# Moving the deferred second half of the output epilogue behind the first block of the Wo projection

## The chip, the cores and the metric

The kernel runs as one program on the eight cores of one Trainium2 chip. Each core takes half of the sequence of one of four batch entries; the cores exchange nothing. The metric is the device time of the slowest core in microseconds (us), as the median of the runs.

## The reference

One recurrent layer over x of shape (4, 4096, 2048): a layernorm, a linear attention with grouped keys and values, a feed-forward net with sign weights, and a gated sum.

```python
def recurrent_layer(x, ...):
    xn = _layernorm(x, axis=-1)
    # attention: q, k, v projections; sq, sk = elu + 1; per head
    kv = jnp.einsum('bhsd,bhse->bhde', sk, v)
    qkv = jnp.einsum('bhsd,bhde->bhse', sq, kv)
    k_sum = sk.sum(axis=2)
    norm = jnp.einsum('bhsd,bhd->bhs', sq, k_sum)
    s = (qkv / (norm[..., None] + EPS))...reshape(b, s, H * D) @ Wo.T
    # feed-forward with sign weights
    hidden = relu(einsum('bsd,hd->bsh', xn, sign(up_weight)) * up_scale)
    out = einsum('bsh,dh->bsd', hidden, sign(down_weight)) * down_scale * output_scale
    return x + s * silu(out)
```

## The kernel before

A first phase normalises the sequence, builds the small attention state and stores converted weights to DRAM. The second phase, `phase_c`, runs over four token blocks of 512 tokens (`tau` 0 to 3). A block has four stages, and TensorE goes through them in this order:

1. Q and attention: 16 heads, `emit_q` (L608) and `emit_attn_tail` (L648 to L688). The last instruction is VectorE's product into `attn_t` (L688).
2. Wo: eight output blocks `ntb` of 256 columns, each with four groups `sub` of 128 tokens. A group is 16 matmuls (L742) into one of only two PSUM buffers, `PS[6]` and `PS[7]`, and one evacuation by ScalarE into `s_tile` (L752). Group number `gidx = 4*ntb + sub`; group g waits for the evacuation of group g-2 (L735 to L739). The weights of a block, 1024 KB, come by a DMA issued on GpSimd's queue (`emit_wo_load`, L715). There are two weight buffers, so the load for block n+2 waits for the last group of block n (L714), and it is emitted at the end of block n.
3. Up: 64 blocks of 16 matmuls (L817), evacuated by ScalarE (L823); weights come by GpSimd's queue (L806).
4. Down: two halves of 1024 output columns (L875, L919, L965), each followed by an epilogue made in `_dn_evac`.

The epilogue has eight pieces i = 0 to 7 of 128x512. The evacuation to `t1_all` (L1030) is made at once. `phase2a` is silu (L1041) and the product with `s_tile` (L1047). `phase2b` adds the residual rows of x and stores the result: for each piece, VectorE's sum into `yt` (L1060), GpSimd's store DMA (L1067), and then, on ScalarE's queue, the load of the x rows of piece i+3 (`emit_xr_load`, L1014 to L1016). Buffers tie these together. `xr` has three slots, so the load for piece i+3 waits for sum i; `yt` has two, so sum i waits until the store of piece i-2 has landed (L1058 to L1059).

For the first half of the columns both parts run at once. For the second half they are kept for the next block: `phase2a` is emitted in front of head 2 of the next Q stage (L694 to L697), and `phase2b` is `pending_ph2b`, emitted after the loads of Wo blocks 0 and 1 and ahead of the first Wo group (L721 to L723). This happens in blocks tau 1, 2 and 3; tau 0 has nothing pending, and that of the last block runs at the very end (L986 to L989).

Each engine executes its instructions in program order, with waits on counting semaphores in the same stream. A DMA is issued by an engine (SP, ScalarE or GpSimd), in order with everything else on that engine. So where `pending_ph2b` is emitted sets its place in three streams: VectorE's, ScalarE's and GpSimd's.

```python
W("vector", S[f"XR{r['slot']}"], r["xr_done"])
if self.yw_done[p4]:
    W("vector", S[f"YW{p4}"], self.yw_done[p4])
... sum L1060, then
W("gpsimd", S["VE"], S["VE"].v)
... store L1067, then
if i + NXR < 8:
    emit_xr_load(i + NXR)     # W("scalar", S["VE"], xr_free[slot]); DMA on ScalarE's queue
```

Of the kernel before, what the change touches and what calls it, by code (L numbers as in the profile page):

```python
# [41 lines left out]
class Builder:  # L42
# [25 lines left out]
    def W(self, eng, sem, v=None):  # L68
        if v is None:
            v = sem.v  # L70
        if v <= 0:
            return
        self.prog.emit(eng, lambda e, h=sem.h, v=v: e.wait_ge(h, v))

    def OP(self, eng, fn, *incs):
        pairs = []
        for s, n in incs:
            s.v += n
            pairs.append((s.h, n))

        def cl(e, fn=fn, pairs=pairs):
            inst = fn(e)
            for h, n in pairs:
                inst = inst.then_inc(h, n)

        self.prog.emit(eng, cl)
# [398 lines left out]
    def phase_c(self, scope):  # L485
# [101 lines left out]
        for tau in range(NTC):  # L587
# [120 lines left out]
            def emit_wo_load(ntb):  # L708
                osl = ntb % 2
                wo = S[f"WO{osl}"]  # L710
                prevs = s_pe.get((tau, ntb - 2, 3)) if ntb >= 2 else (
                    s_pe.get((tau - 1, NTB - 2 + ntb, 3)) if tau >= 1 else None)
                if prevs:
                    W("gpsimd", S["PE"], prevs)  # L714
                OP("gpsimd", lambda e, d=wo_sl[osl], n=ntb: e.dma_start(  # L715
                    d[:], D["woS"][n, :, :]), (wo, 16))
                wo_done[ntb] = wo.v

            emit_wo_load(0)
            emit_wo_load(1)  # L720
            if getattr(self, "pending_ph2b", None) is not None:  # L721
                self.pending_ph2b()
                self.pending_ph2b = None  # L723
            for ntb in range(NTB):
                osl = ntb % 2
                W("tensor", S[f"WO{osl}"], wo_done[ntb])
                if ntb == 0:
                    W("tensor", S["VE"], attn_done_ve)
                    if tau >= 1:
                        W("tensor", S["VE"], self.dn_evac_ve[6])  # L730
                        W("tensor", S["VE"], self.dn_evac_ve[7])
                for sub in range(4):
                    gidx = ntb * 4 + sub
                    psl = PS[6 + (gidx % 2)]
                    war = s_evac_se.get((tau, gidx - 2)) if gidx >= 2 else (  # L735
                        s_evac_se.get((tau - 1, NTB * 4 - 2 + gidx)) if tau >= 1
                        else None)
                    if war:
                        W("tensor", S["SE"], war)  # L739
                    for h in range(H):  # L740
                        OP("tensor", lambda e, h=h, sub=sub, p=psl, w=wo_sl[osl]:
                           e.matmul(p[:, 0:256],  # L742
                                    attn_t[:, h * 512 + sub * 128:
                                           h * 512 + (sub + 1) * 128],
                                    w[:, h * 256:(h + 1) * 256],
                                    start=(h == 0), stop=(h == H - 1)),
                            *(((S["PE"], 1),) if h == H - 1 else ()))
                    s_pe[(tau, ntb, sub)] = S["PE"].v
                    W("scalar", S["PE"], S["PE"].v)
                    if gidx == 0 and tau >= 1:  # L750
                        W("scalar", S["VE"], self.last_stile_ve)
                    OP("scalar", lambda e, sub=sub, n=ntb, p=psl: e.copy(  # L752
                        s_tile[:, sub * DM + n * 256: sub * DM + (n + 1) * 256],
                        p[:, 0:256]), (S["SE"], 1))
                    s_evac_se[(tau, gidx)] = S["SE"].v
                if ntb + 2 < NTB:
                    emit_wo_load(ntb + 2)
            s_pe[(tau, "end")] = S["PE"].v

            if tau == 1:  # L760
# [377 lines left out]
```

How the kernel before makes its waits and increments, by code:

```python
    def W(self, eng, sem, v=None):  # L68
        if v is None:
            v = sem.v
        if v <= 0:
            return
        self.prog.emit(eng, lambda e, h=sem.h, v=v: e.wait_ge(h, v))
# [7 lines left out]
        def cl(e, fn=fn, pairs=pairs):  # L81
            inst = fn(e)
            for h, n in pairs:
                inst = inst.then_inc(h, n)
```

## Time and profile before

| | |
|---|---|
| time before, median of 2 runs | 3877.58 us (3875.78 to 3879.38) |
| time of the profiled execution | 3889.14 us |
| its span, core 5 (the slowest) | 3887.3 us |
| spans of the eight cores | 3831.2 to 3887.3 us |
| TensorE matmul busy | 2941.6 us, 76% of the span |
| ScalarE, VectorE, GpSimd busy | 18%, 14%, 6% |
| DMA | 543.42 MB, mean 140 GB/s |

The profile is of one execution, on the slowest core. Its own time is 11.6 us above the median of the runs; its span is 1.8 us below its own time. Times in the rows are counted from the span's start. In a line of the timeline the first number is a start, the second a length, both in us; `xN` is how many instructions were merged into the line, and the bracket holds the idle time before it on that engine and what ended it. `PE` is TensorE's matmuls, `DVE` VectorE, `ACT` ScalarE, `POOL` GpSimd, `ACTq` the DMAs that ScalarE issues.

### The profile page before, as it was taken

What the parts mean: (1) busy time and instruction counts of PE and PEld (TensorE: products, weight loads), DVE (VectorE), ACT (ScalarE), POOL (GpSimd) and SP (SyncE); (2) the same over time, 40 slices, a digit from 0 to 9 for tenths busy, and PEclk for the clock granted to TensorE, in tenths of its full rate; (3) what the DMA queues carried; (4) which work ended last, traced back from release to release, by engine and by line L of the source; (5) the groups of instructions that cost most, each with busy time, mean ns of one, the idle gap of its engine ahead of it and who ended that gap; (6) DMA issues with size and microseconds to landing.
All of it is one profiled execution on the core that took longest, in us unless ns stands there. A gap on an engine that the chain in (4) does not pass through costs nothing.

```text
span 3887.3 us, 35031 instructions; the slowest of 8 cores (3831.2 to 3887.3 us)
## 1 busy us (share of the span) xinstructions
PE 2941.6 (76%) x13326; PEld 1312.3 (34%) x13326; DVE 534.3 (14%) x870; ACT 706.1 (18%) x982; POOL 239.6 (6%) x454
## 2 busy tenths in 40 slices
PE   4777868777555577688888777788887867888885
PEld 1333326322211133263333332533332325433332
DVE  2554410111111201100000111100001111000011
ACT  1222232223211202321110012211100132111000
POOL 0000000100011000001100000011000000110000
PEclk9988989899877788789999897899998988999998
DMA  6789213898999852133345531333446313334453
GB/s 136 217 231 231 86 54 103 189 196 193 201 213 214 204 159 84 60 119 128 125 127 151 167 94 49 128 114 129 128 130 195 98 54 114 123 130 128 130 156 106
DMA packets 170178, 543.42 MB, mean 140 GB/s; under 512 B 16112, under 2 KB 16144, under 8 KB 159520
## 3 DMA queue, kind: packets, MB, share of 16 engines
q0 software_dynamic: 59744, 239.16, 26.5%
q1 hardware_dynamic: 79168, 201.35, 17.6%
q10 hardware_dynamic: 31104, 100.68, 7.1%
q8 instruction: 111, 1.82, 0.2%
q14 instruction: 51, 0.42, 0.0%
HBM read 520.15 MB, written 109.05 MB: 162 GB/s over the span
## 4 chain that ended last, share of the span: by engine, by line
PE 46%; DMA 27%; ACT 7%; issue 5%; DVE 2%; ACTq 0%; DVEq 0%; SPq 0%; POOLq 0%; POOL 0%
PE psc L817 18%; DMA dn_sl<-dnS 12%; PE psc L965 10%; PE psc L608 8%; DMA dnS<-dn_sl 6%; DMA up_sl<-upS 6%; PE psc L742 6%; PE psc L674 2%; PE psc L919 2%; DMA upS<-up_sl 2%; ACT dn_sl L852 2%; ACT up_sl L786 1%; ACT r_tmp L662 1%; ACT r_row L666 1%; ACT qb L618 1%
## 5 line engine op out<-in xcount | busy, mean ns | idle before, releaser
L817 PE MATMUL psc<-xn_t,up_sl 128*128 128x512 bf16 x4096 | 939.5, 386 | 200.5 <-ACT up_sl L786 90.6
L965 PE MATMUL psc<-dn_sl,hidden 128*128 128x512 bf16 x3072 | 708.6, 388 | 138.0 <-DMA dn_sl<-dnS 109.8
L817 PEld LDWEIGHTS psc<-xn_t,up_sl 128*128 128x128 bf16 x4096 | 393.2, 99 | 745.5 <-issue 324.3
L965 PEld LDWEIGHTS psc<-dn_sl,hidden 128*128 128x128 bf16 x3072 | 295.4, 99 | 551.3 <-issue 238.7
L823 ACT ACTIVATE hidden<-psc,uscb 128x512 bf16<-128x512 f32 x256 | 176.2, 688 | 907.0 <-PE psc L817 907.0
L608 PE MATMUL psc<-xn_t,wq_sl 128*128 128x512 bf16 x1024 | 330.0, 496 | 5.3 <-DVE t_all L1030 3.6
L1030 DVE TENSOR_TENSOR t_all<-psc,dsb 128x512 f32<-128x512 f32 x64 | 39.0, 680 | 1804.1 <-PE psc L965 1678.2
L875 PE MATMUL psc<-dn_sl,hidden 128*128 128x512 bf16 x512 | 171.6, 498 | 148.9 <-ACT dn_sl L852 83.3
L742 PE MATMUL psc<-wo_sl,attn_t 128*128 128x256 bf16 x2048 | 241.0, 283 | 31.0 <-ACT s_tile L752 22.1
L674 PE MATMUL psc<-r_row,ones_r 1*128 1x512 f32 x128 | 89.7, 787 | 202.7 <-ACT r_row L666 202.7
L742 PEld LDWEIGHTS psc<-wo_sl,attn_t 128*128 128x128 bf16 x2048 | 206.9, 101 | 70.3 <-issue 39.4
L608 PEld LDWEIGHTS psc<-xn_t,wq_sl 128*128 128x128 bf16 x1024 | 119.9, 122 | 242.1 <-issue 192.8
L618 ACT ACTIVATE qb<-psc,bq_tb 128x512 f32<-128x512 f32 x64 | 44.0, 688 | 710.4 <-PE psc L608 706.6
L919 PE MATMUL psc<-dn_sl,hidden 128*128 128x512 bf16 x512 | 123.3, 401 | 36.3 <-DMA dn_sl<-dnS 27.8
L875 PEld LDWEIGHTS psc<-dn_sl,hidden 128*128 128x128 bf16 x512 | 55.9, 117 | 264.6 <-issue 240.9
L806 POOL DMA_DIRECT2D up_sl<-upS x192 | 101.3, 528 | 702.3 <-PE psc L817 692.7
L397 PE MATMUL ps_k<-wkb,xn_fm 128*128 128x512 bf16 x512 | 133.8, 421 | 0.8 <-DVE xn_fm L379 0.8
L1067 POOL DMA_DIRECT2D y<-yt x64 | 34.7, 542 | 1599.9 <-DVE yt L1060 1596.5
L406 PE MATMUL ps_v<-wvb,xn_fm 128*128 128x512 bf16 x512 | 115.7, 379 | 0.0
L852 ACT ACTIVATE dn_sl<-t_all 128x2048 bf16<-128x2048 bf16 x32 | 61.1, 1910 | 254.5 <-DMA dnS<-dn_sl 250.4
L674 PEld LDWEIGHTS psc<-r_row,ones_r 1*128 1x128 f32 x128 | 22.8, 221 | 220.1 <-issue 220.1
L752 ACT CAST s_tile<-psc 128x256 bf16<-128x256 f32 x128 | 47.4, 373 | 223.5 <-PE psc L742 182.1
(81 smaller groups left out, 1359.2 us busy)
## 6 DMA issues: line engine op xcount, KB each, us to landing
dn_sl<-dnS SPq DMA_DIRECT2D x224, 512.0 KB, 4.0
up_sl<-upS POOLq DMA_DIRECT2D x192, 512.0 KB, 3.6
wq_sl<-wqS SPq DMA_DIRECT2D x64, 512.0 KB, 3.3
wo_sl<-woS POOLq DMA_DIRECT2D x32, 1024.0 KB, 5.8
t_all<-up_pre POOLq DMA_DIRECT2D x64, 512.0 KB, 8.5
upS<-up_sl ACTq DMA_DIRECT2D x64, 512.0 KB, 6.0
t_all<-dn_pre POOLq DMA_DIRECT2D x64, 512.0 KB, 10.2
dnS<-dn_sl ACTq DMA_DIRECT2D x64, 512.0 KB, 8.5
```

The costliest lines, as they stand in the source:

```text
L397: OP("tensor", lambda e, dc=dc, x=xn_fm[sl]: e.matmul(ps_k[:, 0:KD], x[:, dc * 128:(dc + 1) * 128], wkb[:, dc * KD:(dc + 1) * KD], start=( ...
L406: OP("tensor", lambda e, dc=dc, x=xn_fm[sl]: e.matmul(ps_v[:, 0:KD], x[:, dc * 128:(dc + 1) * 128], wvb[:, dc * KD:(dc + 1) * KD], start=( ...
L608: OP("tensor", lambda e, dc=dc, w=wq_sl[fsl], p=pq: e.matmul(p[:, :], w[:, dc * 128:(dc + 1) * 128], xn_re[:, :, dc, :], start=(dc == 0), ...
L674: OP("tensor", lambda e: e.matmul(PS[5][:, :], P["ones_r"][:], r_row[:], start=True, stop=True), (S["PE"], 1))
L742: e.matmul(p[:, 0:256], attn_t[:, h * 512 + sub * 128: h * 512 + (sub + 1) * 128], w[:, h * 256:(h + 1) * 256], start=(h == 0), stop=(h == ...
L806: OP("gpsimd", lambda e, d=up_sl[usl], j=j: e.dma_start(d[:], D["upS"][j, :, :]), (up, 16))
L817: OP("tensor", lambda e, dc=dc, w=up_sl[usl], p=pu: e.matmul(p[:, :], w[:, dc * 128:(dc + 1) * 128], xn_re[:, :, dc, :], start=(dc == 0), ...
L823: OP("scalar", lambda e, j=j, p=pu: e.activation(hidden[:, j * 512:(j + 1) * 512], p[:, :], AF.Relu, scale=P["usc"][:, j:j + 1]), (S["SE"] ...
L852: e.sign(ap[:], b[:]), (S["SE"], 1))
L875: d=dn_sl[dsl]: e.matmul(PS[b][:, :], hidden[:, j * 512 + sub * 128: j * 512 + (sub + 1) * 128], d[:, ntd * 512:(ntd + 1) * 512], start=(j ...
L919: ntd=ntd, b=bank, d=dn_sl[dsl]: e.matmul(PS[b][:, :], hidden[:, j * 512 + sub * 128: j * 512 + (sub + 1) * 128], d[:, j2 * 1024 + ntd * 5 ...
L965: ntd=ntd, b=bank, d=dn_sl[dsl]: e.matmul(PS[b][:, :], hidden[:, j * 512 + sub * 128: j * 512 + (sub + 1) * 128], d[:, j2 * 1024 + ntd * 5 ...
```

## The change

The three lines that emit `pending_ph2b` are moved from ahead of the loop over the Wo blocks to the end of its first pass. In program order they now stand behind the four groups of block 0, their four evacuations on ScalarE, and the load of Wo block 2 on GpSimd's queue. Nothing else is changed; no instruction is added or removed, and TensorE's and SP's streams are as before.

```diff
             emit_wo_load(0)
             emit_wo_load(1)
-            if getattr(self, "pending_ph2b", None) is not None:
-                self.pending_ph2b()
-                self.pending_ph2b = None
             for ntb in range(NTB):
...
                     s_evac_se[(tau, gidx)] = S["SE"].v
                 if ntb + 2 < NTB:
                     emit_wo_load(ntb + 2)
+                if ntb == 0 and getattr(self, "pending_ph2b", None) is not None:
+                    self.pending_ph2b()
+                    self.pending_ph2b = None
             s_pe[(tau, "end")] = S["PE"].v
```

## Rows read from the trace of the kernel before

**Rows 1.** The page: span, and busy time by engine.

```profile
span 3887.3 us, 35031 instructions; the slowest of 8 cores (3831.2 to 3887.3 us)
PE 2941.6 (76%) x13326; PEld 1312.3 (34%) x13326; DVE 534.3 (14%) x870; ACT 706.1 (18%) x982; POOL 239.6 (6%) x454
```

**Rows 2.** Line L742: what ended its engine's idle time (us, times).

```profile
  ACT s_tile L752: 22.1, 3
  DMA wo_sl<-woS: 1.0, 1
```

**Rows 3.** Timeline, start of the Wo stage of tau 1.

```profile
1671.30 5.78 PE L742 MATMUL psc<-wo_sl,attn_t 128*128 128x256 bf16 x32 [2.02 <-DVE attn_t L688]
1671.47 12.71 ACTq L1016 DMA_DIRECT2D xr<-x_own  x5
1671.97 1.15 POOL L1067 DMA_DIRECT2D y<-yt  x2 [291.06 <-DVE yt L1060]
1676.70 1.29 DVE L1060 TENSOR_TENSOR yt<-t_all,xr 128x512 f32<-128x512 f32 x2 [4.71 <-DMA y<-yt]
...
1684.33 0.65 ACT L752 CAST s_tile<-psc 128x256 bf16<-128x256 f32 x2 [14.33 <-DVE yt L1060]
...
1684.85 17.40 PE L742 MATMUL psc<-wo_sl,attn_t 128*128 128x256 bf16 x138 [7.78 <-ACT s_tile L752]
...
1689.32 0.54 POOL L1067 DMA_DIRECT2D y<-yt  x1 [0.28 <-issue]
1690.77 0.37 ACT L752 CAST s_tile<-psc 128x256 bf16<-128x256 f32 x1 [1.89 <-PE psc L742]
```

**Rows 4.** Timeline, the same place in tau 2.

```profile
2464.04 5.36 PE L742 MATMUL psc<-wo_sl,attn_t 128*128 128x256 bf16 x32 [2.02 <-DVE attn_t L688]
...
2469.54 0.69 DVE L1060 TENSOR_TENSOR yt<-t_all,xr 128x512 f32<-128x512 f32 x1 [4.81 <-DMA y<-yt]
...
2476.98 18.26 PE L742 MATMUL psc<-wo_sl,attn_t 128*128 128x256 bf16 x147 [7.58 <-ACT s_tile L752]
```

**Rows 5.** Timeline, the same place in tau 3.

```profile
3244.52 5.93 PE L742 MATMUL psc<-wo_sl,attn_t 128*128 128x256 bf16 x32 [1.99 <-DVE attn_t L688]
...
3249.51 1.29 DVE L1060 TENSOR_TENSOR yt<-t_all,xr 128x512 f32<-128x512 f32 x2 [4.25 <-DMA y<-yt]
...
3257.15 13.42 PE L742 MATMUL psc<-wo_sl,attn_t 128*128 128x256 bf16 x96 [6.70 <-ACT s_tile L752]
```

**Rows 6.** Timeline, start of the Wo stage of tau 0, which has no epilogue in it.

```profile
609.39 30.82 PE L742 MATMUL psc<-wo_sl,attn_t 128*128 128x256 bf16 x259 [1.67 <-DVE attn_t L688]
...
615.43 0.37 ACT L752 CAST s_tile<-psc 128x256 bf16<-128x256 f32 x1 [2.01 <-PE psc L742]
...
618.93 0.37 ACT L752 CAST s_tile<-psc 128x256 bf16<-128x256 f32 x1 [1.37 <-PE psc L742]
619.38 0.53 POOL L715 DMA_DIRECT2D wo_sl<-woS  x1 [169.68 <-PE psc L742]
...
622.42 0.37 ACT L752 CAST s_tile<-psc 128x256 bf16<-128x256 f32 x1 [1.37 <-PE psc L742]
```

**Rows 7.** DMA view: issue to landing, first up load behind a Wo load, tau 1 to 3.

```profile
up_sl<-upS POOLq DMA_DIRECT2D x1, 512.0 KB, 7.2
...
up_sl<-upS POOLq DMA_DIRECT2D x1, 512.0 KB, 6.3
...
up_sl<-upS POOLq DMA_DIRECT2D x1, 512.0 KB, 6.9
```

**Rows 8.** DMA view: an up load alone (1743.7 us); fastest and slowest store pairs.

```profile
up_sl<-upS POOLq DMA_DIRECT2D x1, 512.0 KB, 3.4
...
y<-yt POOLq DMA_DIRECT2D x2, 256.0 KB, 2.3
...
y<-yt POOLq DMA_DIRECT2D x2, 256.0 KB, 9.2
```

## The prediction

> **What bounds the kernel now.** I read the page first, for the size of things: TensorE is busy 76% of a span of 3887.3 us and no other engine over 18% [rows 1]. So a change in the order of small work can only matter where TensorE is idle because of it. The edit touches the first microseconds of the Wo stage of tau 1, 2 and 3, so I next asked what line L742 waits for. Over the whole kernel its matmuls wait 22.1 us, in three waits, for the evacuation L752, and 1.0 us once for a weight load [rows 2]. Three waits in three blocks with a pending epilogue: that is the place, and 22.1 us (0.6% of the time) is all that any placing of the epilogue can win there. Last I read the timeline at the three places [rows 3 to 5] and at the same place in tau 0, which has no epilogue and is thus the picture of an undisturbed start [rows 6].
>
> The timeline of tau 1 [rows 3] shows the mechanism. Take TensorE's first Wo matmul as 0. Sums 0 and 1 are made at once. Store 0 is issued at +0.67 (1671.97). Sum 2 waits for its landing and starts at +5.40 (1676.70), so store 0 costs 4.73 us from issue to the next sum. Sum 4 waits in the same way for store 2. ScalarE's queue holds the five loads of x rows in front of the evacuation of group 0; the last of them waits for sum 4. ScalarE is therefore stuck until +13.03 (1684.33, idle 14.33 us, ended by L1060). TensorE finished groups 0 and 1 at +5.78 and has no PSUM buffer for group 2; it resumes at +13.55 (1684.85) after 7.78 us. The others are alike: resumed at +12.94 with 7.58 us idle, and +12.63 with 6.70 [rows 4, 5]. The mean resumption is +13.04, the mean stall 7.35 us. From the first matmul to sum 2 it is 5.40, 5.50 and 4.99, mean 5.30; from sum 2 to resumption 8.15, 7.44 and 7.64, mean 7.74 [rows 3 to 5].
>
> The stall is thus not a matter of work but of a chain: store 0 lands, sum 2, store 2 lands, sum 4, last x load, evacuation. The question is when this chain starts, and how much TensorE has in front of it.
>
> **The change part by part.**
>
> *VectorE.* Its stream has nothing between the last `attn_t` product and the sums, before and after. Sums 0 and 1 run at the same time as now. Cost nothing; nothing is queued behind the later sums until the next down epilogue, hundreds of us later.
>
> *GpSimd.* This is the part that decides. The stores now stand behind the load of Wo block 2, and that load waits for the last group of block 0. In tau 0 it is issued at +9.99 (619.38 against 609.39) and takes 0.53 us to issue [rows 6]. Store 0 follows at about +10.6 instead of +0.67: the whole chain starts 9.9 us later, though its data is ready at the same time as now.
>
> *ScalarE.* Four evacuations now go ahead of the five x loads. Loads 3 and 4 are issued right after the evacuation of group 3, the third must wait for sum 2 and the last for sum 4. So groups 0 to 3 are free of the epilogue, and with two PSUM buffers TensorE may also run groups 4 and 5. In tau 0 the evacuation of group 5 starts at +13.03 (622.42) [rows 6]; a group's matmuls end a little ahead of its evacuation (group 1: evacuated at +6.04 in tau 0 [rows 6], ended at +5.78 in tau 1 [rows 3]). TensorE is out of work at +12.9. The cover grows from 5.7 us to 12.9, by 7.2.
>
> *The first store.* The chain starts later by 9.9 and the cover grows by 7.2; already this is a loss of 2.7 us a block. Besides, store 0 (256 KB) is now issued 0.6 us behind a load of 1024 KB on the same queue. The trace has no store in that place. It has the next best thing, the first up load, issued 0.6 us behind the last Wo load: 7.2, 6.3 and 6.9 us to landing [rows 7], against 3.4 alone [rows 8]. Being behind a Wo load costs 3.8, 2.9 and 3.5, mean 3.4 us. I take that for the store too: from issue to sum 2, 4.63 (5.30 less 0.67) + 3.4 = 8.0 us. Bounds: below, no cost, 4.63 us, since the load could be moved beside the store's latency; above, the slowest stores of the trace, 9.2 [rows 8]. I take the up load because it is the row with the same queue, the same distance and the same load in front.
>
> In the Trainium skill, DMA: Bandwidth & Descriptors, section "Anatomy of one DMA", gives a GpSimd DMA 2.0 us plus its bytes over 436 GB/s. By that formula 1024 KB ahead in the queue are an estimated 2.4 us instead of 3.4, and the whole sum would come to +15 us instead of +18. The up rows above speak for the larger number; no store in this trace decides it.
>
> *Sum of a block.* Sum 2 at 10.6 + 8.0 = +18.6; resumption 7.74 later, +26.4, since store 2 is issued when the Wo load has landed and meets the traffic it meets now. The stall is 26.4 - 12.9 = 13.5 us instead of 7.35: +6.1 a block. With the bounds for the store, 4.63 and 9.2, it is +2.7 and +7.3.
>
> *What stays equal.* The two groups after the stall take 5.8 us instead of the 3.5 of later ones (the evacuation of group 3 starts at 1690.77, 5.9 after resumption [rows 3]). This is paid once a block now, for groups 2 and 3, and would be paid once then, for groups 6 and 7; groups 2 to 5 run at the pace of tau 0 [rows 6]. Cost nothing; a stall twice as long could keep TensorE slow for one group more, 1.75 us a block or 5 in all.
>
> *What is late next.* Behind store 7 stands a Wo load: now that of block 2, then that of block 3. Store 7 is issued 4.5 us after resumption (1689.32), and the load needs the second group after it, 5.8. So the load is held by TensorE and not by the stores, as now, and has a block of 7 us to land in. Cost nothing. The load of block 2 is early: it has the stall as cover. All that follows in the block hangs on TensorE, and nothing waits at a fixed time, so a longer stall goes through in full.
>
> *Total.* 3 x 6.1 = +18 us, from 3 x 2.7 = +8 to 3 x 7.3 = +22. Against its own execution that is 3889.14 + 18 = 3907. The profiled execution is 11.6 us above the median of the runs; its stalls are no part of that, and the forecast is 3877.6 + 18 = 3896.
>
> **The rivals.**
>
> *The cover works (faster).* What the edit looks like: six groups instead of two run ahead of the blocked queue, so the stall of 7.35 us goes. It would, if the stores went on at +0.67: sum 2 at +5.3, sum 4 at about +11, and ScalarE free at about +12.5, when TensorE still has work until +12.9. The time would be 3878 - 22 = 3856. Against it is the order of GpSimd's stream. It decides itself at the issue of the first store: every microsecond later than about +0.7 comes back as stall, and the gain is used up when it is issued 7.2 us later, at +7.9. The wait for the last group of block 0, at +9.9, is beyond that.
>
> *The stall only moves.* If store 0 and store 2 land faster in their new place, the chain shortens. At the fastest landing of the trace, 2.3 us [rows 8], for both, where store 2 now takes about the 4.7 of store 0, the stall would be 10.6 + 2.3 + (7.74 - 2.4) - 12.9 = 5.3 us, 2 less than now, and the time 3878 - 6 = 3872; with only part of that it is 3878, no change. For it: 2.3 us is seen. Against it: that pair had no other transfer beside it, and here two x loads and a Wo load are in flight.
>
> *Wo weights come late too (slower still).* If the three landings in the chain took 9.2 us [rows 8], resumption would be 1.2 + 4.5 = 5.7 us later (9.2 against 8.0, and against the 4.7 of now), and stores 6 and 7, behind the third landing, 4.5 us later against resumption. Of that the load of block 3 can lose about 2 us (its store-side time of 5.0 against 5.8, and a landing of about 6 us, less than the 7.2 of [rows 7], in a block of 7), so it would be 2.5 us late. That gives 18 + 3 x (5.7 + 2.5) = +43, 3921. For it: a wait for a Wo load of 1.0 us is already there once [rows 2]. Against it: the first store at this place takes under 5 us in all three blocks [rows 3 to 5].
>
> **How the numbers follow.** The forecast of +8 to +22 has a chance of 0.74, the stall that only moves 0.13, the cover that works 0.06, the late weights 0.07. The forecast's own range is 3886 to 3900; runs differ by some us in themselves (3875.78 to 3879.38 in two runs, and 3889.14 in a third), so I take 3879 to 3912. Below it lie the cover that works and half of the stall that moves, above it the late weights: about 0.19 in all. About 2%, 78 us, is what a measurement of this kernel can tell from no change. None of the cases reaches it, the largest being 43 us. I leave 0.01 for faster and 0.03 for slower, for a mechanism I have not seen.
>
> **What the profile after should show.** At the start of the Wo stages of tau 1 to 3: the Wo load (L715) at about +10 and the first store right behind it at +10.6; six groups of matmuls, out of work at +12.9; the evacuation of group 4 released by the sum at about +26; three waits of L742 for L752 of together some 40 us (30 to 44) instead of 22.1; the first store taking about 8 us to the next sum. Stores issued before +8, or a sum of waits under 22, would refute the main step. A sum of waits as forecast with an unchanged time would mean that something behind it absorbs a stall, which I deny. Waits of L742 for `wo_sl` of several us would show the third rival.

## The result, and the profile after

The changed kernel is slightly slower: 1.0038 times the kernel before, with a 95% interval of 1.0020 to 1.0055. On the 3889.5 us that the kernel before took in the same comparison this is +15 us (+8 to +21); the median of the changed kernel is 3907.44 us over 27 runs. The forecast was +18 us.

The profiled execution of the changed kernel was one of the slow ones, in which all cores are granted a lower clock (0.861 on core 5 against 0.903 before), so its span of 3988.3 us is not to be compared. On core 5, 89 of the 101 us by which it is longer lie ahead of the Wo stage of tau 1; and as a mean of the 24 places below, the six groups ahead of the stall took 12.8 us, where the forecast from rows of the kernel before had 12.9. So the chain of waits can be read. Because three lines were removed ahead of them, the Wo matmuls are now L739 and their evacuation L749.

Line L739 of the changed kernel, what ended its engine's idle time (us, times); it answers to [rows 2]:

```profile
  ACT s_tile L749: 39.8, 3
  DVE attn_t L688: 7.7, 4
  DMA wo_sl<-woS: 1.8, 1
```

Timeline of the changed kernel, start of the Wo stage of tau 1; it answers to [rows 3]:

```profile
1760.25 12.35 PE L739 MATMUL psc<-wo_sl,attn_t 128*128 128x256 bf16 x96 [2.02 <-DVE attn_t L688]
...
1769.20 0.37 ACT L749 CAST s_tile<-psc 128x256 bf16<-128x256 f32 x1 [1.37 <-PE psc L739]
1769.28 16.52 ACTq L1016 DMA_DIRECT2D xr<-x_own  x5
1769.65 0.53 POOL L715 DMA_DIRECT2D wo_sl<-woS  x1 [293.75 <-PE psc L739]
1770.17 1.09 POOL L1067 DMA_DIRECT2D y<-yt  x2
1778.48 1.29 DVE L1060 TENSOR_TENSOR yt<-t_all,xr 128x512 f32<-128x512 f32 x2 [17.53 <-DMA y<-yt]
...
1785.90 0.65 ACT L749 CAST s_tile<-psc 128x256 bf16<-128x256 f32 x2 [16.32 <-DVE yt L1060]
...
1786.41 8.77 PE L739 MATMUL psc<-wo_sl,attn_t 128*128 128x256 bf16 x58 [13.81 <-ACT s_tile L749]
```

Counted from the first matmul, the Wo load is issued at +9.4 and the first store right behind it at +9.9, where [rows 3] have +0.67. TensorE now runs 96 matmuls (six groups) instead of 32 (two groups) before it is stopped, at +12.35, and then stands 13.81 us instead of 7.78. ScalarE stands 16.32 us behind its x loads instead of 14.33.

How long the store takes is in the DMA view. Issues of the changed kernel at 1770 us, KB and us to landing:

```profile
wo_sl<-woS POOLq DMA_DIRECT2D x1, 1024.0 KB, 8.1
y<-yt POOLq DMA_DIRECT2D x1, 256.0 KB, 8.2
```

The place occurs 24 times in a profile (eight cores, three blocks). Means over the 24 places, with the smallest and the largest, all from the timelines and counted from the first Wo matmul in us; the last two columns are the waits of the Wo matmuls in a whole kernel, as a mean of the eight cores:

| kernel | first store issued | sum 2 starts | from store 0 to sum 2 | TensorE resumes | waits for evacuation | waits for `wo_sl` |
|---|---|---|---|---|---|---|
| before | 0.68 | 5.19 | 4.51 (3.8 to 5.4) | 12.53 | 20.9 | 1.9 |
| changed | 10.33 | 18.56 | 8.22 (7.7 to 9.2) | 26.13 | 40.0 | 2.6 |

### The profile page after: what moved, and what is told of

It reads as the page before. It is cut to its first block, busy times and chain, and to the rows that moved or that the text cites. A ratio compares the mean times of both kernels' runs of the same rounds, so it can differ in the third digit from the quotient of the medians.

```text
span 3988.3 us, 35031 instructions; the slowest of 8 cores (3936.9 to 3988.3 us)
## 1 busy us (share of the span) xinstructions
PE 3070.4 (77%) x13326; PEld 1349.3 (34%) x13326; DVE 534.5 (13%) x870; ACT 706.0 (18%) x982; POOL 239.1 (6%) x454
## 4 chain that ended last, share of the span: by engine, by line
PE 49%; DMA 25%; ACT 7%; issue 5%; DVE 2%; ACTq 0%; POOL 0%; DVEq 0%; SPq 0%; POOLq 0%
PE psc L817 20%; DMA dn_sl<-dnS 12%; PE psc L965 10%; PE psc L608 8%; DMA dnS<-dn_sl 6%; PE psc L739 6%; DMA up_sl<-upS 5%; PE psc L674 2%; PE psc L919 2%; ACT dn_sl L852 2%; ACT up_sl L786 1%; DMA y<-yt 1%; ACT r_tmp L662 1%; ACT r_row L666 1%; ACT qb L618 1%
## 5 line engine op out<-in xcount | busy, mean ns | idle before, releaser
L817 PE MATMUL psc<-xn_t,up_sl 128*128 128x512 bf16 x4096 | 1005.5, 407 | 195.2 <-ACT up_sl L786 90.6
L817 PEld LDWEIGHTS psc<-xn_t,up_sl 128*128 128x128 bf16 x4096 | 410.6, 103 | 788.7 <-issue 441.3
L608 PE MATMUL psc<-xn_t,wq_sl 128*128 128x512 bf16 x1024 | 341.1, 508 | 5.3 <-DVE t_all L1030 3.6
L739 PE MATMUL psc<-wo_sl,attn_t 128*128 128x256 bf16 x2048 | 250.7, 290 | 49.5 <-ACT s_tile L749 39.8
L739 PEld LDWEIGHTS psc<-wo_sl,attn_t 128*128 128x128 bf16 x2048 | 212.4, 104 | 92.9 <-issue 57.2
L397 PE MATMUL ps_k<-wkb,xn_fm 128*128 128x512 bf16 x512 | 146.9, 452 | 0.8 <-DVE xn_fm L379 0.8
L406 PE MATMUL ps_v<-wvb,xn_fm 128*128 128x512 bf16 x512 | 138.6, 433 | 0.0
L715 POOL DMA_DIRECT2D wo_sl<-woS x32 | 17.0, 532 | 1281.0 <-PE psc L739 1184.8
L749 ACT CAST s_tile<-psc 128x256 bf16<-128x256 f32 x128 | 47.4, 373 | 251.7 <-PE psc L739 204.4
```

Of the source, the lines that this page charges most:

```text
L397: OP("tensor", lambda e, dc=dc, x=xn_fm[sl]: e.matmul(ps_k[:, 0:KD], x[:, dc * 128:(dc + 1) * 128], wkb[:, dc * KD:(dc + 1) * KD], start=( ...
L406: OP("tensor", lambda e, dc=dc, x=xn_fm[sl]: e.matmul(ps_v[:, 0:KD], x[:, dc * 128:(dc + 1) * 128], wvb[:, dc * KD:(dc + 1) * KD], start=( ...
L608: OP("tensor", lambda e, dc=dc, w=wq_sl[fsl], p=pq: e.matmul(p[:, :], w[:, dc * 128:(dc + 1) * 128], xn_re[:, :, dc, :], start=(dc == 0), ...
L739: e.matmul(p[:, 0:256], attn_t[:, h * 512 + sub * 128: h * 512 + (sub + 1) * 128], w[:, h * 256:(h + 1) * 256], start=(h == 0), stop=(h == ...
L817: OP("tensor", lambda e, dc=dc, w=up_sl[usl], p=pu: e.matmul(p[:, :], w[:, dc * 128:(dc + 1) * 128], xn_re[:, :, dc, :], start=(dc == 0), ...
```

## The experiments

Each run is compared with the kernel before on the same chip; ratios are of the times, with 95% intervals. 1% is 39 us. All kernels compute the whole output.

### Which queue makes the stall: e4 and e1

e4 keeps the new place on ScalarE's queue, but the stores are emitted ahead of the Wo load and so do not wait for group 3:

```diff
-                if ntb + 2 < NTB:
-                    emit_wo_load(ntb + 2)
                 if ntb == 0 and getattr(self, "pending_ph2b", None) is not None:
                     self.pending_ph2b()
                     self.pending_ph2b = None
+                if ntb + 2 < NTB:
+                    emit_wo_load(ntb + 2)
```

> The changed kernel with the epilogue ahead of the Wo load of block 2 at the end of block 0: ScalarE's stream as changed, GpSimd's as before. Theory: waits for the evacuation about 7.5 us in all, but the Wo load is now behind eight stores whose chain starts late for sums 3 to 7: issued at about +26, landed +31, when TensorE wants it at +19: 12 us a block, 37 in all for wo_sl. Sum of both 45 against 23 before: about +22 us, 1.0055. Rival (only the evacuation waits count): 15 us faster, 0.996.

Measured: 1.0041 (1.0002 to 1.0079). The waits for the evacuation are 10.0 us instead of 40.0, those for `wo_sl` 27.2. Timeline of e4, tau 1, slowest core:

```profile
1646.47 12.91 PE L739 MATMUL psc<-wo_sl,attn_t 128*128 128x256 bf16 x96 [2.02 <-DVE attn_t L688]
1647.14 1.15 POOL L1067 DMA_DIRECT2D y<-yt  x2 [283.07 <-DVE yt L1060]
1649.58 0.69 DVE L1060 TENSOR_TENSOR yt<-t_all,xr 128x512 f32<-128x512 f32 x1 [2.41 <-DMA y<-yt]
...
1661.76 5.13 PE L739 MATMUL psc<-wo_sl,attn_t 128*128 128x256 bf16 x32 [2.37 <-ACT s_tile L749]
...
1669.38 1.07 POOL L715 DMA_DIRECT2D wo_sl<-woS  x2
1677.24 13.87 PE L739 MATMUL psc<-wo_sl,attn_t 128*128 128x256 bf16 x105 [10.36 <-DMA wo_sl<-woS]
```

With the same place on ScalarE's queue as in the changed kernel, the stall for the evacuation is 2.37 us here and not 13.81. So it was the late first store, not ScalarE's order, that made the stall long. What was won came back as 10.36 us at block 2, whose weights now stand behind eight stores. As a mean this wait is 9.1 us a block, less than the 12 expected.

e1 takes the stores off GpSimd's queue instead. It is the changed kernel with the deferred stores issued by SP, on semaphores of their own:

```diff
-                W("gpsimd", S["VE"], S["VE"].v)
-                OP("gpsimd", lambda e, r0=r["row0"], c=r["dcol"], p4=p4:
+                yeng, ysem = (("sync", S[f"YH{p4}"]) if dhalf == 1
+                              else ("gpsimd", S[f"YW{p4}"]))
+                W(yeng, S["VE"], S["VE"].v)
+                OP(yeng, lambda e, r0=r["row0"], c=r["dcol"], p4=p4:
```

> The changed kernel, but the eight stores of the deferred half go on SP's queue: they no longer stand behind the Wo load; the five x loads still stand behind four evacuations on ScalarE. Theory (the late start of the stores is what made the stall longer): store 0 at +0.7 again, sum 2 at +5.3; x loads 3 and 4 at +9.6, landing 3.5 later, so sum 3 at about +13 and ScalarE free at +15, against TensorE out of work at +12.9: waits for the evacuation 3 x 2.5 = 7.5 us instead of 40; time 15 to 22 us below the kernel before, 0.9945 to 0.996. Rival (the place in ScalarE's queue makes the stall): waits stay near 40, time as the changed kernel, 1.004.

Measured: 0.9965 (0.9933 to 0.9998), a gain of 14 us against before. The waits for the evacuation are 16.0 us, not 40 and not the 7.5 expected. Over the 24 places sum 3 starts at +12.9, as expected (it waits 9.86 us for its x load below). The next x load is late: it is issued at +9.7 and lands at +15.9, 6.2 us later and not 3.5, so sum 4 and with it ScalarE come late. With 6.1 us for `wo_sl` the waits come to 22.1, about the 22.8 of the kernel before. By its waits this kernel should only have been even with it. The missing 13 to 14 us are taken up below (e9).

```profile
1649.44 12.36 PE L739 MATMUL psc<-wo_sl,attn_t 128*128 128x256 bf16 x96 [2.02 <-DVE attn_t L688]
...
1662.41 0.69 DVE L1062 TENSOR_TENSOR yt<-t_all,xr 128x512 f32<-128x512 f32 x1 [9.86 <-DMA xr<-x_own]
...
1665.86 19.45 PE L739 MATMUL psc<-wo_sl,attn_t 128*128 128x256 bf16 x160 [4.06 <-ACT s_tile L749]
```

### The price of the Wo load in front of the store: e3

In e3 GpSimd waits for group 3 as in the changed kernel, then issues the stores, and the Wo load behind them:

```diff
-                if ntb + 2 < NTB:
-                    emit_wo_load(ntb + 2)
                 if ntb == 0 and getattr(self, "pending_ph2b", None) is not None:
+                    W("gpsimd", S["PE"], s_pe[(tau, 0, 3)])
                     self.pending_ph2b()
                     self.pending_ph2b = None
+                if ntb + 2 < NTB:
+                    emit_wo_load(ntb + 2)
```

> The changed kernel, but GpSimd first waits for the last group of block 0 and then issues the stores, with the Wo load behind them. The chain starts as late as in the changed kernel (+10.05), but no Wo load is in front of store 0. Theory: store 0 to sum 2 takes 4.6 us again instead of 8; TensorE resumes at +22.4, waits for the evacuation 3 x 9.5 = 29 us instead of 40; wo_sl is late by about 5 us a block, 15 in all; total about +21 us against before. If the landing of store 0 had nothing to do with the Wo load in front, the waits for the evacuation stay near 40.

Measured: 1.0107 (1.0070 to 1.0143). The evacuation waits fall to 29.4 us, as expected. Over the 24 places store 0 to sum 2 takes 5.44 us (3.8 to 7.8), against 8.22 with the Wo load in front and 4.51 before. So of the 3.7 us that the store costs more in the changed kernel 2.8 are due to the Wo load on its own queue, and 0.9 to something else, which was not separated.

The total was twice what I expected, 41 us instead of 21. The timeline shows both reasons:

```profile
1692.19 5.89 PE L739 MATMUL psc<-wo_sl,attn_t 128*128 128x256 bf16 x32 [10.48 <-ACT s_tile L749]
...
1697.20 0.54 POOL L715 DMA_DIRECT2D wo_sl<-woS  x1
...
1698.64 0.54 POOL L715 DMA_DIRECT2D wo_sl<-woS  x1 [0.90 <-PE psc L739]
1704.95 9.05 PE L739 MATMUL psc<-wo_sl,attn_t 128*128 128x256 bf16 x57 [6.88 <-DMA wo_sl<-woS]
1708.62 0.37 ACT L749 CAST s_tile<-psc 128x256 bf16<-128x256 f32 x1 [10.08 <-PE psc L739]
1711.37 0.37 ACT L749 CAST s_tile<-psc 128x256 bf16<-128x256 f32 x1 [2.38 <-PE psc L739]
```

Two Wo loads are in flight together, the first lands in 7.7 us, and the wait is 6.88 (7.7 as a mean, about 5 expected). And each of the two stalls is followed by a slow pair of groups. At the second it is 6.4 us from resumption to the second evacuation (6.0 as a mean of the 24 places), where it is 3.75 behind short waits of e2 that left the granted clock at 1.00. I had counted the pair once. 29.4 + 23.1 - 22.8 = 30 us of waits and 3 x 2.3 = 7 us of slow groups make 37 of the 41.

### Does more work in front help: e6

```diff
-                if ntb == 0 and getattr(self, "pending_ph2b", None) is not None:
+                if ntb == 1 and getattr(self, "pending_ph2b", None) is not None:
```

> The changed kernel with the epilogue at the end of block 1 instead of block 0, behind the Wo load of block 3. Theory: the start of the chain and the work in front of it both move by 7 us, so the stall is the same 13.5 us a block: waits for the evacuation about 40 us, ratio 1.004. Rival (more matmuls in front of the queue hide more): 8 groups in front, stall 7 us a block shorter, about 19 in all, ratio about 0.999.

Measured: 1.0067 (1.0047 to 1.0086), 26 us; 1.004 was expected. By its waits (39.6 for the evacuation and 2.7 for `wo_sl`, 22.8 before) it should be 19.5 us, the low end of that interval. Ten groups run before the stall instead of six, and the waits for the evacuation are 39.6 us (changed kernel: 40.0); the first store is issued at +17.2 and sum 2 comes 8.2 us later. The stall does not depend on the place, because the start of the chain moves with the cover. Timeline of e6, tau 1:

```profile
1663.90 19.75 PE L739 MATMUL psc<-wo_sl,attn_t 128*128 128x256 bf16 x160 [2.02 <-DVE attn_t L688]
...
1681.23 1.09 POOL L1067 DMA_DIRECT2D y<-yt  x2
1689.43 1.30 DVE L1060 TENSOR_TENSOR yt<-t_all,xr 128x512 f32<-128x512 f32 x2 [24.82 <-DMA y<-yt]
...
1697.03 11.51 PE L739 MATMUL psc<-wo_sl,attn_t 128*128 128x256 bf16 x80 [13.37 <-ACT s_tile L749]
```

### Both queues freed: e5 and e2

e5 is the kernel before with the five deferred x loads on SP:

```diff
-                    emit_xr_load(i + NXR)
+                    emit_xr_load(i + NXR, "sync" if dhalf == 1 else "scalar")
```

> The kernel before, with only the five x loads of the deferred half on SP's queue; stores on GpSimd's, in the old place. Theory: ScalarE is free, no wait of L742 for the evacuation (22 us before); but the stores still hold GpSimd until about +18.5 and the Wo load of block 2 behind them lands at +24, when TensorE wants it at +16.4: 8 us a block, 23 in all for wo_sl. The stall has changed its name; ratio 1.000. Rival (ScalarE alone is the cause): 22 to 29 us faster, 0.993.

Measured: 1.0070 (1.0046 to 1.0094), slower than expected. The evacuation waits are gone (0.5 us), but those for `wo_sl` are 39.6 us and not 23. The waits thus grew by 17 us, and the time by 27 (18 to 36); the other 10 are open. e5 moved something that I had left out. SP's queue also carries the first two loads of the down weights, which had been issued ahead of the Wo stage. They now stand behind the x loads and fall onto the third pair of stores. The DMA view of e5, issues from 1666 to 1669 us, and the sum behind them:

```profile
dn_sl<-dnS SPq DMA_DIRECT2D x2, 512.0 KB, 8.1
y<-yt POOLq DMA_DIRECT2D x2, 256.0 KB, 8.1
```

```profile
1675.84 0.69 DVE L1060 TENSOR_TENSOR yt<-t_all,xr 128x512 f32<-128x512 f32 x1 [7.75 <-DMA y<-yt]
...
1679.00 1.07 POOL L715 DMA_DIRECT2D wo_sl<-woS  x2
1684.95 14.23 PE L742 MATMUL psc<-wo_sl,attn_t 128*128 128x256 bf16 x112 [14.61 <-DMA wo_sl<-woS]
```

e2 has both the x loads and the stores on SP (the edits of e5 and e1, on the kernel before).

> Epilogue in the old place; in the deferred half the five x loads and the eight stores go on SP's queue instead of ScalarE's and GpSimd's. Theory (the loss is a chain that blocks ScalarE's and GpSimd's queues): no wait of L742 for its evacuation (22 us before, 40 after), Wo load of block 2 issued about 10 us after the first Wo matmul, no slow pair of groups after a stall (3 x 2.3 us less); 22 + 7 = 29 us faster than the kernel before, ratio 0.9925. Rival (a stall here is absorbed further on, and the loss of the change comes from elsewhere): waits gone, time within 5 us of the kernel before.

Measured: 0.9920 (0.9874 to 0.9966). No wait for the evacuation is left (0.4 us), and 9.1 us for `wo_sl`. The stall is thus worth its time; it is not absorbed further on. But 22.8 - 9.5 = 13 us of waits and 7 us of slow groups are 20 us, and 31 were measured. As in e1, that is more than the waits explain, here by some 11 us.

### The end of the kernel: e9

The missing part lies behind the last matmul. From its end to the end of the span it is 39.7 us before (38.3 to 40.6 over the cores), 39.5 changed, 39.2 in e5, but 28.2 in e1 and 28.1 in e2: the last epilogue is a deferred one too, and its stores went to SP. e9 changes only that, on the kernel before:

```diff
+                yeng, ysem = (("sync", S[f"YH{p4}"])
+                              if dhalf == 1 and tau == self.NTC - 1
+                              else ("gpsimd", S[f"YW{p4}"]))
```

> The kernel before; only the eight stores of the very last epilogue (the second half of tau 3, behind the last matmul) go on SP's queue instead of GpSimd's. Question: with the stores on SP the time from the last matmul's end to the end of the span was 28.5 us, with GpSimd 39 to 40. Theory (two gains were mixed in the runs with stores on SP: the Wo stages, and this end): Wo stages as before, waits of L742 for the evacuation about 22 us, the end 11 us shorter, ratio 0.997. Rival (the end is short for another reason, such as the order of earlier loads): end stays at 39 us, ratio 1.000.

Measured: 0.9969 (0.9940 to 0.9998), 12 us, with the end at 27.6 us and the evacuation waits unchanged at 20.9. Here is the end in e9, core 5, and then in the kernel before:

```profile
3844.32 1.29 DVE L1062 TENSOR_TENSOR yt<-t_all,xr 128x512 f32<-128x512 f32 x2
3845.08 13.68 SPq L1071 DMA_DIRECT2D y<-yt  x8
3845.09 8.34 ACTq L1018 DMA_DIRECT2D xr<-x_own  x5
3848.74 0.69 DVE L1062 TENSOR_TENSOR yt<-t_all,xr 128x512 f32<-128x512 f32 x1 [3.13 <-DMA y<-yt]
```

```profile
3858.92 1.28 DVE L1060 TENSOR_TENSOR yt<-t_all,xr 128x512 f32<-128x512 f32 x2
3860.16 1.14 POOL L1067 DMA_DIRECT2D y<-yt  x2 [118.24 <-DVE yt L1060]
3864.57 1.32 DVE L1060 TENSOR_TENSOR yt<-t_all,xr 128x512 f32<-128x512 f32 x2 [4.37 <-DMA y<-yt]
```

From the first sum to the third it is 4.42 us with SP and 5.65 with GpSimd, partly issue (0.76 against 1.24 from the sum's start) and partly landing. But these steps are the smaller part. As means over the cores, from the first sum to the issue of the last store it is 14.4 us in e9 and 17.5 before, 3.1 less; from there to the end of the span it is 2.4 us and 11.4, 9.0 less. What fills the 11.4 us is GpSimd's last instruction. The view of line L35, which closes each of the program's two blocks on every engine, has two of them on GpSimd, an early one and the last. A line gives the shortest, the median and the longest in ns, then the start of each in us; the last is the shorter one. Before, core 5, and then e9:

```profile
L35 POOLq DRAIN  x2: 8547/12123/15699, 363.7 to 3878.5; - x2
```

```profile
L35 POOLq DRAIN  x2: 7894/11570/15247, 372.2 to 3736.5; - x2
```

With its last store on GpSimd, the kernel ends with a `DRAIN` of 8.55 us on GpSimd, which starts when that store has landed; it is 8.55 us on all eight cores, before, in the changed kernel and in every run whose last stores come from GpSimd. In e9 GpSimd's last DMA is issued over 130 us before the end on every core, and its `DRAIN` of 7.89 us is over long before TensorE has finished. So of the 12.1 us 8.55 are this `DRAIN` out of the way, 3.1 the shorter chain and some 0.5 a quicker last landing (2.1 us instead of 2.6). What the `DRAIN` waits for no run shows.

### Out of the Wo stage altogether: e7, e8, and both gains together: e10, e11, e12

GpSimd stands idle through the whole Q stage (the 291 us in [rows 3]). e7 puts one piece of the deferred half at each of heads 4 to 11; `phase2b` takes a piece number, and the x load of a later piece is issued one head after its slot was freed:

```diff
                 emit_q(f)
+                if f >= 4 and tau >= 1 and self.piece_i < 8:
+                    self.pieces(self.piece_i)
+                    self.piece_i += 1
...
+                if only is not None and i >= 1 and i - 1 + NXR < 8:
+                    emit_xr_load(i - 1 + NXR)
```

> The kernel before, with the deferred sums, loads and stores of tau 1 to 3 spread over the next Q stage: one piece at each of heads 4 to 11, sum behind the head's product on VectorE, x load of piece i+2 on ScalarE, store on GpSimd, nothing left in the Wo stage. The last epilogue as before. Theory: the Wo stage starts as in tau 0, no wait for the evacuation, about 1 us for wo_sl in all: 22 us of stall and 7 us of slow groups saved. Eight sums of 0.69 us fit into VectorE's idle 2.6 us ahead of each attn_t product; five issues of 0.35 us on ScalarE a block may cost up to 5 us in all. Ratio 0.9925 to 0.994. Rival (the Q stage is a chain over all engines and what is put into it lengthens it): Q stages longer by 8 x 0.7 us a block, 17 us in all, ratio 0.997.

Measured: 0.9894 (0.9862 to 0.9927), 41 us, more than the 23 to 29 expected. In the profiles the three Wo stages give 28 of them (58.3 us each against 67.7 in e9, which ran on the same chip and has the epilogue in the old place). The down stages of tau 1 to 3 are shorter too, by 7, 6 and 2 us; why was not shown. Timeline of e7, core 5: a piece inside a head, then the start of the Wo stage.

```profile
1598.27 0.69 DVE L634 SCALAR_TENSOR_TENSOR sq_sl<-qb,e_q 128x512 bf16<-128x512 f32 x1 [0.89 <-ACT e_q L627]
1598.76 0.63 ACT L667 ACTIVATE r_row<-r_tmp 1x512 f32<-1x512 f32 x1
1598.88 0.69 DVE L1066 TENSOR_TENSOR yt<-t_all,xr 128x512 f32<-128x512 f32 x1
...
1600.12 0.54 POOL L1073 DMA_DIRECT2D y<-yt  x1 [9.13 <-DVE yt L1066]
```

```profile
1658.24 31.92 PE L744 MATMUL psc<-wo_sl,attn_t 128*128 128x256 bf16 x271 [2.02 <-DVE attn_t L689]
```

The sum runs behind `sq_sl` without a wait for its buffers, and the Wo stage starts with 271 matmuls in one piece, where it was broken after 32 [rows 3]. Waits for the evacuation are 0.0 us, for `wo_sl` 0.7. The Q stages are no longer than before: on core 5, from the first head's `negq` to the last `attn_t`, 160.6, 160.6 and 163.2 us against 162.2, 164.2 and 161.2.

e8 is e7 with all the deferred stores on SP (with the edit of e1).

> As the run with one piece per head, and the stores of the deferred half, those of the last epilogue too, on SP's queue. Theory: both gains add: 29 us in the Wo stages and 11 us at the end, ratio 0.9895 to 0.991. Rival: the stores on SP hold up the loads of Wq behind them in the Q stage, waits of L608 for wq_sl appear, ratio 0.995.

Measured: 0.9918 (0.9896 to 0.9941), the end at 28.0 us and no wait for `wq_sl`, but not faster than e7. Three more kernels ran on one chip to separate this: e10 is e7 with only the last stores on SP (the edit of e9), e11 is e7 again, e12 is e8 again.

> One piece per head in the Q stage with stores on GpSimd, and the stores of only the last epilogue on SP's queue: the two separate gains put together. Theory (they add): 29 to 41 us in the blocks and 11 us at the end, 40 to 52 in all, ratio 0.987 to 0.990, and 11 us below the kernel with one piece per head. Rival (stores on SP cost something elsewhere, which would explain that the version with all deferred stores on SP was not faster): no better than one piece per head alone, 0.9894 or above.

> The kernel with one piece per head again, on the same chip as the other two. If both gains add, 11 us above each of the versions with the last stores on SP; ratio 0.9894 to 0.9925.

> One piece per head with all deferred stores on SP, again. If its 0.9918 was a chance of the runs, it comes out equal to the version with only the last stores on SP, 0.987 to 0.990; if SP's queue costs something in the Q stage, it is 10 us or more above that version.

Measured: e10 0.9843 (0.9824 to 0.9862), e11 0.9888 (0.9846 to 0.9929), e12 0.9917 (0.9889 to 0.9944). e10 is the fastest version, 61 us below the kernel before, and better than both kernels of the case. It is 17 us below e11, where 11 was expected, but the intervals of the two overlap, so this does not tell 17 from 11. e12 repeats the result of e8, and its interval lies clear of that of e10: all deferred stores on SP do cost something against e10, 29 us by the ratios. Where is open. The profiles, one execution of each, are only 15 us apart (means over the cores). e12 needs 1047 us from the Wo stage of tau 0 to that of tau 1 against 1037 of e10; 8 of these 10 us lie in the down stage of tau 0, ahead of the first deferred store, where both run the same program. Behind that it is 767.5, 768.4 and 620.2 us from one Wo stage to the next and to the end, against 765.1, 764.1 and 618.9. The Q stages are equal within 1 us, so the cost that was expected there is not seen.

## Why the prediction was right

Point by point, with the changed kernel's 24 places:

- *Where the chain starts.* Forecast +10.6, measured +10.33. This is the step that decided, and e4 and e1 confirm it from two sides: with the stores free of the wait the evacuation waits fall from 40 us to 10 and 16.
- *The cover.* Forecast: out of work at +12.9; measured 12.8 as a mean, 12.35 in tau 1 on core 5. e6 shows that more cover bought in this way is worth nothing.
- *The first store.* Forecast 8.0 us to sum 2, measured 8.22. The up load behind a Wo load [rows 7, 8] was a good stand-in. The make-up was a little different: I took 3.4 us for the Wo load in front, and e3 gives 2.8, with 0.9 for other traffic. That the one error nearly makes up for the other is luck. The estimate from the Trainium skill, DMA: Bandwidth & Descriptors, section "Anatomy of one DMA", was 2.4 us. It is nearer to the 2.8 of e3 alone; for the whole 3.7 us that the store costs more, the row was nearer.
- *The rest of the chain.* From sum 2 to resumption 7.74 forecast, 26.13 - 18.56 = 7.57 measured.
- *The total.* Waits for the evacuation 40 us forecast, 40.0 measured; resumption +26.4 against +26.13. The time was 15 us longer (8 to 21), forecast 18. The median of 3907.44 us is 11 above the 3896 forecast, since the kernel before took 3889.5 us in this comparison and not the 3877.6 of the two runs that I started from. The evacuation waits grew by 19.1 us, within that interval, so nothing behind the stage was shown to absorb or add.
- *The rivals.* The working cover is refuted by the store's place in the timeline and by e6. The stall that only moves: the chain from the first store on became longer, not shorter. Late Wo weights: 2.6 us of waits against 1.9, in the changed kernel no matter; e3, e4 and e5 show that mechanism at 23 to 40 us once the load stands behind the stores.

One assumption was taken too easily, without harm: that what stands behind a stall costs nothing more. e3 shows a second stall in the same stage bringing a second slow pair of groups, 2.3 us each time. In the changed kernel there is still one, and it takes 6.0 us to the second evacuation against 5.8 before: a stall twice as long did not slow a third group.

## What to carry to other kernels

Where deferred work is moved behind more work in order to hide a queue that it blocks, find the first link of its chain and look at what its issue now waits for on *its* queue; here the edit moved the start by 9.7 us and the cover by 7.2. Work that consists of short steps and long landings is best given one step at a time to a stage in which its queues are idle, as in e10. Look also at which engine issues the last DMA of the kernel (e9). And a queue that is lent to other work (SP in e5) shifts its own prefetches too: list them first.

## What the runs showed of the hardware that I had not expected

- A store of 256 KB takes 2.5 us from issue to the next sum when only the next store is in flight with it (e4, mean of 24 places), and 4.51 with two x loads of 256 KB issued by ScalarE just ahead (before). Issued by SP it takes 2.4 us alone (e1) and 2.8 with the same loads behind it on SP's queue (e2). Much of what I had read as the store's own latency in [rows 3] was other traffic.
- Behind the last matmul, stores issued by SP instead of GpSimd shorten the end from 39.7 to 27.6 us (e9): 8.55 us because GpSimd's closing `DRAIN` no longer follows the last store, 3.1 through shorter steps of the chain and 0.5 through a quicker last landing. How much of the 3.1 is the issue and how much the order among the transfers was not separated.
- The slow pair of groups costs about the same after a stall of 6.9 us as after one of 13.3 (5.8 and 6.0 us to the second evacuation, means of 24 places before and changed). In the kernel before TensorE's granted clock is 0.50, its lower level of 1.2 GHz, from resumption at 1684.9 to 1689.3 us, and 1.00 (2.4 GHz) from 1690.7 on. e2 has eight waits of 2.7 to 4.0 us in its Wo stages; behind six of them the clock stays at 1.00 and the second evacuation comes after 3.75 us, behind two it comes after 5.4.
